# Slot experts: the first layer as three fp32r products of high and low parts

## What is computed

```python
xn = rmsnorm(x, norm_gamma)
sn = rmsnorm(slot_embeds, slot_norm_gamma)
logits = jnp.einsum('bnd,esd->bnes', xn, sn)
dispatch = jax.nn.softmax(logits, axis=1)
combine = jax.nn.softmax(logits.reshape(b, n, e * s), axis=-1)
slots = jnp.einsum('bnd,bnes->besd', xn, dispatch)
h = jnp.einsum('besd,edh->besh', slots, w1) + b1[None, :, None, :]
h = jax.nn.gelu(h, approximate=False)
eo = jnp.einsum('besh,ehd->besd', h, w2) + b2[None, :, None, :]
out = jnp.einsum('bmd,bnm->bnd', eo.reshape(b, e * s, DIM), combine)
```

## Time and profile before

| | |
|---|---|
| Median of 3 runs | 956.55 us (956.08 to 961.22) |
| Profiled execution, its own time | 957.64 us |
| Its span, first to last instruction | 955.9 us |
| TensorE busy | 832.8 us (87%) |
| VectorE busy | 695.7 us (73%) |
| ScalarE busy | 551.9 us (58%) |
| GpSimd busy | 528.1 us (55%) |
| Mean granted TensorE clock | 0.969 |

### The profile page before, as it was taken

One profiled execution on the slowest core, in us unless ns is written; L12 is line 12 of the kernel. 1 busy time (PEld: TensorE's weight loads), 2 busy tenths in 40 slices (PEclk: granted clock), 3 DMA queues, 4 the chain that ended last, 5 costly groups with the idle time before them and its releaser, 6 DMA issues.

```text
span 955.9 us, 18784 instructions
## 1 busy us (share of the span) xinstructions
PE 832.8 (87%) x6902; PEld 557.0 (58%) x6902; DVE 695.7 (73%) x1450; ACT 551.9 (58%) x1027; POOL 528.1 (55%) x577
## 2 busy tenths in 40 slices
PE   7689997999899999999997779787899968999990
PEld 4356664448644444444443547464667648999980
DVE  5889984003789999999993699999677435657475
ACT  6566665430288788888876464545786543433320
POOL 2500005907089888888532279998057752656572
PEclk9999999999999999999999799999999998999995
DMA  5012210236121221121210998000111121332396
GB/s 163 1 45 88 89 45 23 67 132 198 25 36 36 36 35 36 26 35 36 36 25 1 155 211 244 1 1 0 45 36 53 36 76 36 97 109 89 96 252 205
DMA packets 109899, 70.65 MB, mean 74 GB/s; under 512 B 41538, under 2 KB 103436, under 8 KB 108272
## 3 DMA queue, kind: packets, MB, share of 16 engines
q1 hardware_dynamic: 99440, 60.11, 25.2%
q0 software_dynamic: 4608, 6.64, 2.1%
q10 hardware_dynamic: 5760, 2.70, 1.0%
HBM read 32.04 MB, written 31.60 MB: 67 GB/s over the span
## 4 chain that ended last, share of the span: by engine, by line
PE 46%; DVE 27%; POOL 7%; issue 7%; ACT 4%; DMA 2%; ACTq 1%; POOLq 0%; SPq 0%; DVEq 0%
PE banks L2217 7%; PE banks L2209 6%; PE banks L2020 5%; POOL rows_dram L946 5%; DVE B_mneg L1147 4%; PE banks L1989 4%; PE banks L2007 3%; PE banks L1966 3%; PE banks L1939 3%; PE banks L1933 3%; DVE D_dmx L1263 2%; DVE D_sc L1290 2%; DVE banks L1313 2%; DVE C_nmax L1085 2%; PE banks L1994 2%
## 5 line engine op out<-in xcount | busy, mean ns | idle before, releaser
L1147 DVE TENSOR_REDUCE B_mneg<-banks 128x2 f32<-128x768 f32 (+1 forms) x128 | 136.4, 1086 | 7.9 <-PE banks L1994 4.3
L1682 ACT ACTIVATE B_pt<-banks 128x768 f32<-128x768 f32 (+1 forms) x128 | 117.1, 916 | 30.8 <-PE banks L2007 28.7
L829 POOL TENSOR_SCALAR_AFFINE_SELECT B_pt<-B_pt 128x512 f32<-128x512 f32 x128 | 80.4, 636 | 83.4 <-ACT B_pt L1682 62.1
L2020 PE MATMUL banks<-B_pt,B_vp 128*32 128x512 f32 (+3 forms) x1024 | 95.7, 444 | 0.5 <-POOL B_pt L829 0.2
L1813 ACT ACTIVATE F_gh<-banks 128x512 f32<-128x512 f32 (+1 forms) x96 | 49.4, 527 | 80.1 <-PE banks L2209 75.9
L972 POOL DMA_INDIRECT y_dram<-F_yo,F_ide x60 | 62.3, 1038 | 59.3 <-DVE F_yo L1508 42.1
L946 POOL DMA_INDIRECT rows_dram<-F_xs,F_rowi x64 | 62.5, 976 | 51.3 <-issue 51.0
L2217 PE MATMUL banks<-F_gw,F_gh 128*128 128x128 f32 x640 | 75.2, 275 | 0.0
L1989 PE MATMUL banks<-B_kt,B_qt 64*128 64x256 bf16 (+3 forms) x512 | 73.3, 303 | 1.7 <-ACT B_pt L1682 1.2
L2217 PEld LDWEIGHTS banks<-F_gw,F_gh 128*128 128x128 f32 x640 | 73.9, 192 | 0.6
L2007 PE MATMUL banks<-B_qt,B_kt 64*128 64x256 bf16 (+3 forms) x512 | 64.6, 302 | 7.4 <-DVE B_mneg L1147 5.3
(11 more groups left out here) (300 smaller groups left out, 2241.0 us busy)
## 6 DMA issues: line engine op xcount, KB each, us to landing
comb_dram<-C_comb SPq DMA_DIRECT2D x6, 1024.0 KB, 3.9
rows_dram<-D_zeros SPq DMA_DIRECT2D x8, 650.0 KB, 16.4
F_xe<-rows_dram SPq DMA_DIRECT2D x8, 650.0 KB, 3.9
C_w<-w_in SPq DMA_DIRECT2D x16, 256.0 KB, 3.1
C_cst<-comb_dram SPq DMA_DIRECT2D x4, 1024.0 KB, 6.7
y_dram<-D_zeros SPq DMA_DIRECT2D x2, 2048.0 KB, 18.4
F_gw<-mw_in SPq DMA_DIRECT2D x16, 256.0 KB, 3.2
F_xs<-y_dram SPq DMA_DIRECT2D x16, 256.0 KB, 4.8
```

Of the source, the lines that this page charges most:

```text
L829: g.affine_select(out=w, in_=w, compare_op=ALU.is_ge, fill=0.0, base=0, pattern=[[0, G], [1, P]], channel_multiplier=-1).then_inc(B_md, 1)
L1147: v.tensor_reduce(mneg[:, g % 2, :, pairs[0], qt_], scores[:, :, 0:w], X, ALU.max, negate=True).then_inc(B_mx, 1)
L1682: a.activation(pt[:, 2 * hp:2 * hp + 2, PT_AT[kt]:PT_AT[kt] + w], scores[:, :, 0:w], ACT.Exp).then_inc(B_ex, 1)
L2020: ins = t_.matmul(bank[7][SL * r:SL * r + SL, kt * P:T], vp[:, g // NG % 2, g % NG, kt, SL * r:SL * r + SL], pt[:, r, PT_AT[kt]:PT_AT[kt] ...
```

## The change

VectorE gets a function `high_and_low(pr, par)` that makes four tiles for one expert: `x_high`, the expert's 512 slot vectors cast to fp32r, `w_high`, its first-layer weights cast to fp32r, and the two rests `x_low` and `w_low` as fp32r. TensorE waits for these (`C_hl`) in place of the weights, and makes three fp32r products in place of one fp32 product for each of the four hidden blocks. The second layer stays as it is. There is one buffer of each of the four tiles. So `high_and_low` of the next expert first waits until all first-layer products of the current one are done (`C_hp`), and until the next expert's weights are in (`C_w`). It stands on VectorE ahead of the `pair` addition of the current expert. The one for expert 0 stands ahead of the two reciprocals, the one for expert 1 behind them. Three of the tiles lie where `C_disp` lies, which is dead by then; `C_x_high` is a new tile behind `C_ones`.

```diff
--- before.py
+++ after.py
@@ -462,7 +462,11 @@
         xgT = C("xgT", [P, 2, T])
         nmax = C("nmax", [P, 4])
         dsums, least = C("dsums", [P, 2, 2]), C("least", [P, 4])
-        disp = C("disp", [P, NT, ES])
+        with ExitStack() as memS:
+            disp = sb("C_disp", [P, NT, ES], at=memS)
+        C("below_parts", [P, 8])
+        x_low, w_high, w_low = (C(name, [P, ES], F32R) for name in ("x_low", "w_high", "w_low"))
+        C("above_parts", [P, ES - 8])
         slotsT = C("slotsT", [P, B, ES])
         w1, w2 = C("w1", [P, 2, HID]), C("w2", [P, 2, NJ, D])
         b1, b2 = C("b1", [P, EXP * NJ]), C("b2", [P, EXP])
@@ -474,6 +478,7 @@
         eo = C("eo", [P, B, 4, D])
         cst = C("cst", [P, 2, 4, T])
         ones_c = C("ones", [P, P])
+        x_high = C("x_high", [P, ES], F32R)
         highest, below = (eo[:, i, :, :].rearrange("p j d -> p (j d)") for i in (0, 3))
         sln, diag = eo[:, 1, :, :], eo[:, 2, :, :]
         C_in = sem("C_weights_in")
@@ -488,6 +493,7 @@
         C_w = [sem("C_w_even"), sem("C_w_odd")]
         C_cw = [sem("C_comb_stored_even"), sem("C_comb_stored_odd")]
         C_hp, C_hs = sem("C_hidden_psum"), sem("C_hidden_sbuf")
+        C_hl = sem("C_high_and_low_parts")
         C_ep, C_es = sem("C_expert_psum"), sem("C_expert_sbuf")
         C_pp, C_ps = sem("C_pair_psum"), sem("C_pair_sbuf")
         C_st, C_op, C_os = [sem(f"C_staged{i}") for i in range(4)], sem("C_out_psum"), sem("C_out_sbuf")
@@ -1110,6 +1116,23 @@
             for it in range(B // 2 - 1):
                 dve_round_c(it, False)
             dve_round_c(B // 2 - 1, False, True)
+            def high_and_low(pr, par):
+
+                e = pr * (2 * SLOTS) + par * SLOTS
+                dve.wait_ge(C_w[par], pr * 32 + 32)
+                if pr or par:
+                    dve.wait_ge(C_hp, at(pr, par, NJ, 0))
+                mine = slotsT[:, :, bass.ds(e, SLOTS)]
+                by_batch = "p (b s) -> p b s"
+                v.tensor_copy(x_high[:].rearrange(by_batch, b=B), mine)
+                own.link(v.tensor_copy(w_high[:], w1[:, par, :]))
+                v.tensor_tensor(x_low[:].rearrange(by_batch, b=B), mine, x_high[:].bitcast(F32).rearrange(by_batch, b=B),
+                                ALU.subtract)
+                v.tensor_tensor(w_low[:], w1[:, par, :], w_high[:].bitcast(F32), ALU.subtract).then_inc(C_hl, 1)
+                dve.wait_ge(C_hl, 2 * pr + par + 1)
+
+            dve.wait_ge(C_ta, c_total("ta"))
+            high_and_low(0, 0)
             dve.wait_ge(A_sd, 1)
             dve.wait_ge(C_ex, c_total("l"))
             v.reciprocal(crs[:], csum[:, 0:TILES]).then_inc(C_crs, 1)
@@ -1120,6 +1143,8 @@
             dve.sem_inc(C_pp, 2)
             for pr in range(EXP // 2):
                 for par in range(2):
+                    if (pr, par) != (EXP // 2 - 1, 1):
+                        high_and_low(pr + par, 1 - par)
                     dve.wait_ge(C_ep, at(pr, par, 1, 1) + 1)
                     if par == 0:
                         dve.wait_ge(C_pp, pr * 2 + 2)
@@ -1927,11 +1952,13 @@
             for pr in range(EXP // 2):
                 for par in range(2):
                     e = pr * (2 * SLOTS) + par * SLOTS
-                    pe.wait_ge(C_w[par], pr * 32 + 32)
+                    pe.wait_ge(C_hl, 2 * pr + par + 1)
                     for j in range(NJ):
                         pe.wait_ge(C_hs, at(pr, par, NJ, j + 1))
-                        t_.matmul(bank[j][:], w1[:, par, j * P:(j + 1) * P], slotsT[:, :, bass.ds(e, SLOTS)],
-                                  start=True, stop=True).then_inc(C_hp, 1)
+                        of_j = slice(j * P, (j + 1) * P)
+                        t_.matmul(bank[j][:], w_high[:, of_j], x_high[:], start=True, stop=False)
+                        t_.matmul(bank[j][:], w_low[:, of_j], x_high[:], start=False, stop=False)
+                        t_.matmul(bank[j][:], w_high[:, of_j], x_low[:], start=False, stop=True).then_inc(C_hp, 1)
 
                     pe.wait_ge(C_es, at(pr, par, 1, 1))
                     for j in range(NJ):
```

## The result

The changed kernel takes 972.9 us in the median of 4 runs (968.99 to 976.83), the kernel before 958.88 (956.08 to 962.13, 4 runs). The ratio is **1.014, with a 95% interval of 1.011 to 1.018**: slower, and by more than the 0.5% that the prediction took as the least that can be told. The forecast was 969.5, with a range of 958.5 to 975 and 0.77 for slower. Of all executions in this document one, of 967.2 us at a mean clock of 0.91, lay far above the others of its kernel, and the ratio of that kernel (the sixth experiment) is formed without it.

A forecast was written before the change was run, and what follows sets the result against it. TensorE was taken to bound the kernel almost without a break. Delays reached +16.4 us at expert 3's first layer, savings left +13.0: 957.64 + 13.0 = 970.6 for the profiled execution, 969.5 us against the median, range 958.5 to 975.

The forecast's parts named there:

- Step 1: Expert 0: TensorE starts 2.0 us later behind the conversion, half of that returns, so +0.4 us.
- Step 2: Expert 1: casts wait behind both reciprocals, `x_high` slips in between GpSimd's memsets, `w_high` waits for the second: +10.5 us.
- about 7 us in one record: Expert 1's `w_high` cast on VectorE would last this long, ending with GpSimd's memset of `B_ks`.
- the sign of being wrong: The forecast is wrong if expert 1's `w_high` cast takes 0.43 us, or expert 1 starts before 168.
- Step 3: Expert 1's first layer at low clock after TensorE's idle time: 5.1 us in place of 3.43, sum +12.2.
- Step 4: Experts 2 and 3: GpSimd's normalisation holds casts and subtractions, conversions take 5.8 us; first layers start +14.6 and +16.4.
- second fall of the clock: Rival: the clock falls again in idle gaps around the transposes at experts 2 and 3; +15.4, 972 us, chance 0.12.
- Step 5: Experts 4 to 7: conversions lie inside the second layer, nothing is added, 2.7 us come back: +13.0.
- Lighter hold: Rival: memsets hold casts, but subtractions pass GpSimd's instructions at experts 2 and 3; +8.3, 965 us, chance 0.10.
- Memsets let both casts through: Rival: expert 1's two casts pass GpSimd's memsets together, no low clock follows; +3.3, 960 us, chance 0.10.
- No hold at all: Rival: casts use VectorE's own path, only the wait for the reciprocals is left; -1.3, 955 us, chance 0.13.

The follow-up runs named there:

- the sixth experiment: Changed kernel plus memsets written as fp32, normalisation let through in threes, and expert 1's own tiles made ahead of the reciprocals: 954.39 us median, 0.9965 to the kernel before.

## Why the prediction was right, and where it was not

Shifts against the kernel before, measured from the start of the last slots' copy, which takes out stage C's scatter:

| point | forecast | measured |
|---|---|---|
| first layer of expert 1 starts | +10.5 | +11.0 |
| second layer of expert 1 | +12.2 | +13.0 |
| first layer of expert 2 | +14.6 | +16.8 |
| first layer of expert 3 | +16.4 | +18.2 |
| stage's end | +13.0 | +15.5 |

Forecast for the median was 13.0 us over the kernel before; measured were 14.0 (972.9 - 958.88). That these lie only 1.0 apart is partly luck: the stage came out 2.5 too long, and single times scatter by some 4 us outside it.

**Step 1, expert 0.** The conversion's own durations came as in the earlier trace rows. That this first layer too runs at low clock was not foreseen: behind 2.98 us of idle time most of its products came 0.43 apart, here and in all nine experiments. In this kernel it cost little, since expert 1 waits for VectorE; that is why expert 1 starts only 0.5 later than forecast.

**Step 2, expert 1.** The size was right, one detail wrong: "the cast of `x_high` at 163.2 waits for its end and slips in" did not happen. It waited for both memsets (8.10 us), and `w_high` took 0.61. So the sign "about 7 us in one record" for `w_high` did not show, and the sign of being wrong, 0.43 us for it, was nearly met although the hold was there: both were tied to the wrong cast. I had carried the turn-taking of the earlier trace rows over to memsets; it held only in the kernel with a semaphore between them. The kernel with short memsets shows the mechanism (stage -8.2), the one with the semaphore that the detail changes nothing.

**Step 3, the clock.** TensorE idle for 8.1 us behind expert 0, then 12 products 0.43 apart, 5.5 us to the end of the last against 5.1 forecast. Right as a description. As a cost the 2.4 us of this spell are not a term of their own: with the spell taken away the clock fell at the next gap, and the stage was as long as before.

**Step 4, experts 2 and 3.** The mechanism was right: casts and subtractions both held, shown by the kernel with the normalisation later. The conversions took 6.2 and 4.8 us where 5.8 was put for each, because the last subtraction of expert 3 met a GpSimd that had nothing more to do. The term that was too small is the one for expert 2, +16.8 against +14.6: the rival "second fall of the clock" happened, in part. Of the 2.2 us, 0.8 were there before (0.5 at expert 1's start, 0.3 in its first layer), 0.4 are the conversion, and 0.9 are the eight transposes, which took 1.97 us in place of 1.09. The first products of expert 2 were 0.43 apart as well. I had given it a chance of its own, 0.12, but its sum came nearer to what was measured than the forecast's.

**Step 5, experts 4 to 7.** From the first layer of expert 3 to the end the forecast gave five savings back, 16.4 to 13.0, or 3.4; measured were 2.6 (18.16 to 15.53). A saving is 0.63, so 3.15 were due. Of the missing 0.5, some 0.3 is the first product of expert 3, which stands at 0.50 in the chain where one in the middle of a layer stands at 0.23. The other 0.2 is at expert 6, where "nothing is added" was too good: the weights' DMA landed 3.95 us after its issue, where the earlier trace rows have a median of 3.2 and a maximum of 4.4, and the `pair` addition behind the conversion began 0.2 late.

**The rivals.** *Lighter hold* falls with the kernel that has the normalisation later: there the subtractions went from 1.5 to 1.7 us back to 0.69, so they had not passed. It is half true for memsets, where the added product passed. *Memsets let both casts through* falls with 8.10 us. *No hold at all* falls too; the reciprocal, which it took as its witness, is again 6.50 us beside a memset.

What part of the 15.5 us is clock and what part is holding was not separated. Removing both holds gives 13.6 back. Of the low-clock spells it takes away only the one behind expert 1 (the transposes and the first products of expert 2); the first layers of experts 0 and 1 still had most products 0.43 apart. Filling a gap with work left the length where it was.

## What to carry to other kernels

Work that is moved onto an idle VectorE is not free when GpSimd is busy beside it: look at what GpSimd does in the very microseconds in which the new casts and two-input instructions fall, and price them by GpSimd's instructions, not by their own. A long memset that nobody waited for can become the longest wait in a stage, and if casts are put ahead of it, it will hold the next ones that come: shorten it (here by writing it as fp32) and let it wait for the casts. When a saving of 0.68 us per step is small against a single wait of 8, first make the waits go; only the version without the long holds was faster than the kernel before.

## What the runs showed of the hardware beyond this

- A waiting cast was passed over by a second GpSimd memset issued right behind the first (8.10 us), but got in when GpSimd waited for a semaphore between the two (1.24 us, then 7.22 for the next cast). In the earlier trace rows, between GpSimd products, VectorE did get its turn each time. What decides between memsets and products is open.
- GpSimd's memset goes by elements, not bytes: the same 128 x 8,192 bf16 tile took 6.93 us as bf16 and 3.52 as 4,096 fp32.
- With fp32 products up to 1.98 us before expert 1, TensorE's granted clock still fell, about a microsecond after the fp32r products had begun (0.86 from 174 to 175 us, 0.50 from 175). With that gap closed to 0.27 us it stayed at the full level, and fell behind the next one, of 3.59 us.
- The same code, stage C up to the last slots, ended at anything from 153.2 to 157.9 us, and stage D's stretch was 261.1 to 268.1 us long. For a change within one stage the length of that stage in the trace tells more than one run's time.
